# A two-layer attention and expert kernel: fourth pair dispatched in front of the turns, bias products in front of the phase products, ten products on ones

## The reference

```
logits = jnp.einsum('GSM,ME->GSE', x, router_w)          # 8 groups of 256 rows, 8 experts
raw = softmax(logits); m1 = one_hot(argmax(raw)); m2 = one_hot(argmax(raw * (1 - m1)))
p1 = cumsum(m1) - m1;  p2 = cumsum(m2) - m2 + m1_count   # a row's place in its expert's list
dispatch = (combine != 0)                                # places under the capacity C = 64
expert_inputs = jnp.einsum('GSEC,GSM->EGCM', dispatch, x)
```

## Time and profile before

| | |
|---|---|
| time, median of 3 runs | 641.67 us (640.97 to 641.88) |
| the profiled execution's own time | 640.19 us |
| its span, first to last instruction | 638.4 us |
| TensorE busy in the span | 584.2 us (92%) |
| VectorE / ScalarE / GpSimd busy | 487.9 / 327.6 / 178.2 us |
| TensorE's granted clock, mean | 0.972 |
| the routing chain, 425.0 to 464.7 us | TensorE busy 33.48 of 39.70 us, granted clock 0.83 |

### The profile page before, as it was taken

The page is one execution under the profiler, slowest core; times in us unless marked ns, Lnnn a source line. Parts: engine busy times, 40 slices in busy tenths (PEclk is TensorE's granted clock), DMA queues, the critical chain, the costliest instruction groups (busy, mean ns, idle before and its releaser), DMA issues. The chain is left out here.

```text
span 638.4 us, 12435 instructions
## 1 busy us (share of the span) xinstructions
PE 584.2 (92%) x4195; PEld 364.3 (57%) x4222; DVE 487.9 (76%) x1174; ACT 327.6 (51%) x587; POOL 178.2 (28%) x162
## 2 busy tenths in 40 slices
PE   2877999999999999899999988888989999999996
PEld 1434544444444545799999953435436666556554
DVE  6789889999989888455555578656778888977465
ACT  2842467575766667555555457762132652263124
POOL 2450000000133432133333310000006677788300
PEclk9888799999999999999999999997899999999999
DMA  8945726060714080211111034224011231411322
GB/s 186 242 128 198 238 69 202 8 207 3 194 51 107 28 236 19 50 50 47 50 46 46 29 93 120 68 57 127 0 45 28 73 79 45 137 60 43 98 63 66
DMA packets 55755, 58.00 MB, mean 91 GB/s; under 512 B 8794, under 2 KB 39546, under 8 KB 55658
## 3 DMA queue, kind: packets, MB, share of 16 engines
q1 hardware_dynamic: 51386, 50.56, 28.6%
q0 software_dynamic: 4320, 6.81, 3.3%
HBM read 41.96 MB, written 18.85 MB: 95 GB/s over the span
## 5 line engine op out<-in xcount | busy, mean ns | idle before, releaser
L754 ACT ACTIVATE arena<-banks 128x512 f32<-128x512 f32 (+1 forms) x304 | 156.3, 584 | 96.8 <-PE banks L1704 54.5
L1723 PE MATMUL banks<-arena 96*128 96x512 bf16 (+3 forms) x384 | 119.3, 341 | 5.8 <-DVE mpart L1185 1.8
L1701 PE MATMUL banks<-arena 128*128 128x512 bf16 (+3 forms) x358 | 106.4, 327 | 5.8 <-ACT arena L754 3.0
L1188 DVE TENSOR_REDUCE mpart<-banks 128x1 f32<-128x512 f32 x128 | 86.1, 685 | 9.7 <-PE banks L1723 8.9
L1185 DVE CUSTOM_DVE_ANT_0 banks<-banks,arena 128x512 f32<-128x512 f32 (+1 forms) x128 | 79.1, 636 | 8.3 <-PE banks L1723 5.6
L1635 PE MATMUL banks<-arena 128*128 128x128 f32 x624 | 76.3, 275 | 1.0 <-ACT arena L695 1.0
L1635 PEld LDWEIGHTS banks<-arena 128*128 128x128 f32 x624 | 72.8, 192 | 1.5 <-ACT arena L695 1.5
L1780 PE MATMUL banks<-arena 128*9 128x512 f32 (+3 forms) x768 | 71.0, 488 | 0.0
L1701 PEld LDWEIGHTS banks<-arena 128*128 128x128 bf16 x384 | 38.0, 100 | 52.3 <-issue 25.6
L797 ACT ACTIVATE arena<-banks 125x512 f32<-125x512 f32 (+2 forms) x48 | 28.5, 595 | 72.1 <-PE banks L1898 57.4
L601 POOL DMA_INDIRECT results<-arena x39 | 37.5, 961 | 88.5 <-DVE arena L1079 88.5
(11 more groups left out here) (293 smaller groups left out, 915.1 us busy)
## 6 DMA issues: line engine op xcount, KB each, us to landing
k_parts<-arena SPq DMA_DIRECT2D x6, 768.0 KB, 8.1
arena<-in_L_ffn_experts_w_dram SPq DMA_DIRECT2D x2, 2048.0 KB, 10.2
arena<-results SPq DMA_DIRECT2D x8, 512.0 KB, 6.9
arena<-k_parts SPq DMA_DIRECT2D x7, 576.0 KB
arena<-q_parts SPq DMA_DIRECT2D x28, 144.0 KB
arena<-in_L_ffn_w_kernel_dram SPq DMA_DIRECT2D x8, 344.0 KB, 3.5
slots<-in_pad_rows_dram SPq DMA_DIRECT2D x1, 2535.0 KB, 12.4
arena<-slots SPq DMA_DIRECT2D x39, 65.0 KB, 1.8
```

The costliest lines, as they stand in the source:

```text
L754: act.activation(Pr[:, r % 4, heads[0]:heads[-1] + 1, 0:n], ring_e[e % 3][:, 0:len(heads) * n].rearrange("p (j c) -> p j c", j=len(heads)) ...
L1188: ins = dve.tensor_reduce(part, ps[:, 0:n], AX_X, ALU.max)
L1701: ins = pe.matmul(ring_e[e % 3][:, at * n:at * n + n], QK[:, slot, j, 1, P * kt:P * kt + P], QK[:, slot, j, 0, q:q + n], start=True, stop= ...
L1723: ins = pe.matmul(ps[:, at * n:at * n + n], QK[0:TALL, slot, j, 0, P * i:P * i + P], QK[0:TALL, slot, j, 1, 512 * half:512 * half + n], st ...
```

## The change

Three edits, all in the routing chain:

1. `dispatch(3)` moves from behind the logits to the place right behind `dispatch(2)`, in front of the turns. On ScalarE `dispatched(3)` moves with it, in front of the copies of the turned rows.
2. The bias products move from behind `places1` to the place right behind the logits, in front of the phase products, and behind the wait for the loads of layer 1 (`ld_L1`).
3. Behind `places1` stand ten new products of `ones_d` by `ones_d` (128x128 each, float32), whose result, in bank 7, nothing reads.

```diff
@@ ScalarE
-            for g in range(3):
+            for g in range(G1 // 2):
                 dispatched(g)
             ...
             route_exp(1)
-            dispatched(3)
             for g in range(G1 // 2, G1):
                 dispatched(g)
@@ TensorE
-            for g in range(3):
+            for g in range(G1 // 2):
                 dispatch(g)
             ...
             ins.then_inc(Z["lg_ps"], 1)
-            dispatch(3)
             pe.wait_ge(Z["ld_L1"], 16 * 6)
+            for o in range(2):
+                for c in range(4):
+                    ins = pe.matmul(psO[:, o:o + 1], W1g[:, c, P * o:P * o + P], vecs[:, 6 + c:7 + c], start=(c == 0), stop=(c == 3))
+            ins.then_inc(Z["cb_ps"], 1)
             for c in (1, 2, 0, 3):
             ...
             places1(1, psM[:, 1, :])
-            for o in range(2):
-                for c in range(4):
-                    ins = pe.matmul(psO[:, o:o + 1], W1g[:, c, P * o:P * o + P], vecs[:, 6 + c:7 + c], start=(c == 0), stop=(c == 3))
-            ins.then_inc(Z["cb_ps"], 1)
+            for _ in range(10):
+                pe.matmul(psO[:, 512:512 + P], ones_d[:, :], ones_d[:, :], start=True, stop=True)
```

## The result

| | before | after |
|---|---|---|
| time, median (lowest to highest), 13 runs each | 640.32 us (637.81 to 643.39) | 638.46 us (636.07 to 642.04) |
| ratio after / before, 95% interval | | 0.9962 (0.9945 to 0.9979) |
| profiled execution's own time | 640.19 us | 637.48 us |
| its span, mean granted clock | 638.4 us, 0.972 | 635.7 us, 0.977 |
| start of the expert loop | 464.69 us | 461.98 us |

The change makes the kernel faster by 0.38% (0.21 to 0.55%), 2.4 us. Between the two profiled executions the loop starts 2.71 us earlier and the time is 2.71 us less: behind the loop's start nothing was given back or added. Stages before the chain vary from run to run, so the rest of this text counts from the start of the turns (438.83 before, 439.04 after). The loop starts 25.86 us behind it before and 22.94 after.

What follows compares the result with a forecast made beforehand. TensorE bounds the kernel behind the routing chain, whose middle is set by TensorE's queue; so the loop's start counts. Counts -0.6 and dispatches -1.7 give -2.3 us, 639.4 us on the median of 641.67; range 636.4 to 642.0.

Steps and rivals of the forecast that it cites:

- The pair in the gap: dispatch(3) fills TensorE's 1.98 us idle before the turns; clock stands through the turns, logits end 1.8 us earlier.
- The bias products: Moved between logits and phase products, they lengthen the narrow stretch; clock falls near 442.4, they run at half clock until 445.8.
- second fall: Clock drop in the last dispatches, 456.3 to 459.7, costing 1.7 us; forecast not to come after the change.
- old cover: Time behind the counts, 2.97 us before dispatch(4), while VectorE makes the places; the bias products hid there.
- The phase products: Behind the bias products; clock back 4.3 us after 445.8 (bounds 3.3 to 5.3), end at 451.4, counts 0.6 us earlier.
- rival 1: The clock stands through the narrow stretch after the logits; gain 5.9 us, 635.8 us; chance 13%.
- The ten ones: Behind the counts, 2.40 us of wide work, 0.6 us idle left; last dispatches take 7.1 us, gaining 1.7.
- first fall: Clock drop before the counts, near 439.2 in the kernel before; forecast to come near 442.4 after the change.
- Rival 2: The ones don't prevent the clock's fall in the last dispatches, or another replaces it; gain 0.6, 641.1 us; chance 19%.
- rival 3: Clock still half when the ones begin, so they delay dispatch(4), 2.5 us late; 644.2 us; chance 8%.
- Rival 4: The pair doesn't keep the clock up, it falls at 439.4 as before; gain 0.8, 640.9 us; chance 8%.
- The sum: Whole routing chain: counts -0.6 and dispatches -1.7 give -2.3 us, 639.4 us on the median.

Runs made afterwards that it cites:

- e4: The changed kernel with dispatch(3) moved back behind the logits; time ratio 1.0055 to the kernel before.
- e6: The kernel before with eight products on ones added behind dispatch(2), in the gap in front of the turns; time ratio 0.9957.
- e5: The kernel before with four products on ones added behind the counts, in front of the bias products; time ratio 0.9972.
- e11: The kernel before with its bias products moved behind dispatch(7), nothing in their old place; one profile, loop 23.71 us behind the start of the turns.
- e3: The changed kernel with the bias products back behind the counts and four products on ones in front of them instead of ten; ratio 0.9910 to the kernel before.
- e12: Same as e3 but with the four products on ones behind the bias products; time ratio 0.9926 to the kernel before.
- e1: The changed kernel with only the pair's move: bias products back behind the counts, no products on ones; time ratio 0.9918 to the kernel before.
- e7: The changed kernel with eight wide products replacing the bias products before the phase products, bias products behind the counts after four ones; ratio 0.9913 to the kernel before.
- e2: The changed kernel without its ten products on ones; time ratio 0.9971 to the kernel before.
- e9: Second profile of the changed kernel without its ten products on ones (e2 again); one profile, loop 21.31 us behind the start of the turns.
- e10: Third profile of the changed kernel without its ten products on ones (e2 again); one profile, loop 22.94 us behind the start of the turns.
- e8: The changed kernel with twenty products on ones instead of ten; one run, 639.61 us.

## Why the prediction was right, step by step

**The pair in the gap: right.** Idle time 0.25 us (forecast 0.2 to 0.5), clock 1.00 at 439.4, logits end 3.42 us behind the turns' start instead of 5.35: -1.9, forecast -1.8. e4 and e6 bear out the reason. In all ten profiles with the gap filled the clock stood for 3.2 us or more from the start of the turns. With the gap open it fell within 0.6 us in three (before, e4, e5) and at 3.3 us in the fourth (e11). So the open gap often brings the early fall, not always. ScalarE's copy was not late.

**The bias products: right in this execution, for a reason that was only half right.** Forecast: a fall near 442.4 and 3.4 us; measured 442.4 to 442.8 and 3.28. The prediction laid the fall to the longer narrow stretch. But with the logits alone in front of the phase products or dispatch(3) it came too, in e3, e6, e11 and e12, 3.2 to 3.9 us behind the start of the turns (3.6 in the changed kernel); only e1 had none before the counts. What goes with the bias products is how long it lasted, 6.8 us instead of 3.4. The evidence it gave, the second fall of before, needed no narrow products, as e11 shows. The price was also larger than the prediction let it look. It took their place on the path as given and worked out the net. e3 shows the alternative that it left unpriced: 3.4 us of loop start, more than the whole gain of the change. Their old cover, 2.97 us for 1.93 us of work, was in the earlier trace rows.

**The phase products: right, with the size at the edge.** Clock back 4.0 us after they began (forecast 4.3, bounds 3.3 to 5.3; the window at 449.2 with its 0.67 puts the first rise of before at 449.5 and not at 449.3, so the upper bound should have been 5.4), counts at 450.94 (forecast 451.4), 1.0 us earlier than before where 0.6 was forecast. The rule of the Trainium skill ("TensorE: Matmul & The Clock Gate", Part 1), that the clock follows how busy TensorE has recently been, read literally gave rival 1. The trace disagrees: behind two short pauses of 0.25 and 0.37 us TensorE was busy without a pause from 440.06, the clock fell at 442.6 and stayed down for 6.8 us, and in e4 it stayed down for 17 us of unbroken busy time. With e7 beside it, the engine's busy time in the profile does not tell what its clock will do.

**The ten ones: the size was right, the cause was not shown.** Forecast 2.40 us of fill, 0.6 us idle, 7.1 us of dispatches, -1.7; measured 2.48, 0.47, 7.13, -1.70. But e2, e9 and e10 have the same 7.13 us without any fill. In the profiles without a fill the second fall followed how long the clock had been back when the counts began: 2.5 us in the kernel before (449.5 to 451.96), 3.5 in e11 (446.6 to 450.05), 2.9 in e6, no fall before in e1: all fell again. 1.2 us in e2 (451.4 to 452.59), 1.5 in e9, 1.9 in e10: none did. In the changed kernel it was 1.5 us (449.4 to 450.94), in e4 and e8 1.0 and 1.1. So it may well be the late end of the first fall, a side effect of the bias products in front, that spared it the second. This is a pattern in seven profiles, not an experiment on its cause, and why it should be so stays open. That a fill can prevent a second fall is likely all the same, from two other runs. In e7 the clock had been back 3.0 us, longer than in two of the profiles that fell, and with four ones in the cover no second fall came. In e5 it was 2.4 us, next to the 2.5 of before, with the same code up to the counts: none came either, and the time of 12 runs fell by 0.28%. Each is one profile.

**Rivals.** Rival 1 (clock stands through) was seen in no profile with narrow products in front; the nearest is e9, where it fell behind them. Rival 2 did not occur, rival 3 neither, though e8 shows the price of a fill that is too long: 1.5 us for ten ones more, at full clock. Rival 4 is in e4 and e5 as the behaviour of an unfilled gap, not with the pair moved.

**The sum.** -2.3 forecast, -2.71 us between the profiles, -2.4 in the ratio of the runs. That -2.3 and -2.4 meet so closely is partly luck: in executions of the same code up to the counts these came 2.9 us apart (before and e11), in e2 and e9 1.6 us, and the forecast took one profile of before as the typical one. The counts gave 1.0 us instead of 0.6, the dispatches 1.7 as forecast, but not shown to be for the reason given. The absolute time, 638.46 for 639.4, is lower since the kernel before measured 640.32 in the longer series, 1.35 us under the three runs that the forecast started from.

## What to carry to other kernels

Price every part of a combined change against its own old place, not only the sum: here the pair's move alone gave 0.82%, and the products moved in front of the phase products gave more than half of it back (e1 to e2, 0.9918 to 0.9971). Work that hides in a cover should stay there; look for the idle time of the waiting engine (3.92 us on VectorE after the change) before calling a chain finished. Where the granted clock falls in a short chain, fill the gap in front of it with real work first (e1), or with products on constants (e6), and behind the counts only up to the length of the cover (e8).

## What the runs showed of the hardware

- Sixteen records of one column took 1.93 us at full clock, 3.28 us mostly at half, and 3.41 (e4) and 3.55 us (e10) all at half, about as long as sixteen of 128 columns (3.32 us, mostly at half, in e7): narrow products are not cheap, and in no profile did the clock come back while products of one or eight columns ran. In the routing chain it always came back within products of 512 columns.
- A fall of the clock before the counts lasted 6.8 us in the four profiles in which the bias products ran inside it and the pair had been moved, and 3.4 us in five in which products of 512 columns did (e3, e6, e9, e11, e12). In e4, with a gap of 1.99 us in front, it lasted 17 us while TensorE was never idle.
- The same code, up to the counts, had its first fall 0.4 us behind the start of the turns in the profile of before and 3.3 us behind it in e11, which moved the counts by 2.9 us. One profile of such a chain is one draw.
- Over 13 runs of one kernel the mean granted clock went from 0.969 to 0.980 and the time from 642.04 to 636.07 us.
